# The causal mask of a head pair in quarters of the array

## The reference

```python
q = jnp.einsum('bsd,hde->bhse', x, Wq)
k = jnp.einsum('bsd,hde->bhse', x, Wk)
v = jnp.einsum('bsd,hde->bhse', x, Wv)
scores = jnp.einsum('bhse,bhte->bhst', q, k)
causal = jnp.tril(jnp.ones((S, S), dtype=bool))
scores = jnp.where(causal, scores / jnp.sqrt(jnp.float32(E)), jnp.float32(-jnp.inf))
attn = jax.nn.softmax(scores, axis=-1)
out = jnp.einsum('bhst,bhte->bhse', attn, v)
heads = out.transpose(0, 2, 1, 3).reshape(B, S, H * E)
y = x + heads @ Wo
```

## Time and profile before

| | us |
|---|---|
| median of 3 runs | 875.02 |
| lowest, highest | 874.08, 876.87 |
| the profiled execution | 875.58 |
| its span in the trace | 873.7 |
| TensorE busy in it | 739.8 |
| VectorE busy | 615.9 |
| ScalarE busy | 569.6 |
| GpSimd busy | 510.6 |

### The profile page before, as it was taken

The page is one execution under the profiler, slowest core; times in us unless marked ns, Lnnn a source line. Parts: engine busy times, 40 slices in busy tenths (PEclk is TensorE's granted clock), DMA queues, the critical chain, the costliest instruction groups (busy, mean ns, idle before and its releaser), DMA issues. The chain is left out here.

```text
span 873.7 us, 20974 instructions
## 1 busy us (share of the span) xinstructions
PE 739.8 (85%) x7592; PEld 530.6 (61%) x7592; DVE 615.9 (70%) x1275; ACT 569.6 (65%) x1567; POOL 510.6 (58%) x496
## 2 busy tenths in 40 slices
PE   4881777742799999999999999999999999999842
PEld 3661556632566767667667767766766776676631
DVE  1361665653476668758987986897798698779973
ACT  1462666652476777677777777777777777677633
POOL 3552555343065566856675785667568567666831
PEclk9986888866899999999999999999999999999975
DMA  7500000000099998889889998898788878999820
GB/s 187 119 1 0 1 1 2 0 0 1 14 144 150 146 148 145 142 142 141 139 144 137 151 144 142 146 146 147 136 146 140 147 142 148 139 144 154 149 57 23
DMA packets 360614, 94.00 MB, mean 108 GB/s; under 512 B 347584, under 2 KB 360384, under 8 KB 360512
## 3 DMA queue, kind: packets, MB, share of 16 engines
q1 hardware_dynamic: 357248, 90.57, 62.5%
q10 hardware_dynamic: 3264, 2.10, 0.8%
HBM read 6.63 MB, written 2.10 MB: 10 GB/s over the span
## 5 line engine op out<-in xcount | busy, mean ns | idle before, releaser
L1004 POOL TENSOR_TENSOR prob_hl<-prob,prob_hl 128x768 f16<-128x768 f32 (+1 forms) x192 | 347.6, 1810 | 208.0 <-DVE prob_hl L944 207.7
L915 ACT ACTIVATE prob<-wide,neg_max 128x128 f32<-128x128 f32 (+3 forms) x512 | 264.5, 525 | 157.1 <-DVE neg_max L956 157.1
L956 DVE TENSOR_REDUCE neg_max<-wide 128x2 f32<-128x256 f32 (+3 forms) x256 | 204.6, 821 | 116.9 <-PE wide L833 116.3
L828 PE MATMUL wide<-k_sb,q_sb 64*128 64x128 f32 (+3 forms) x1024 | 190.1, 469 | 0.9 <-ACT k_sb L810 0.8
L944 DVE CAST prob_hl<-prob 128x768 f16<-128x768 f32 (+1 forms) x192 | 149.0, 776 | 0.6 <-ACT prob L915 0.5
L853 PE MATMUL bank<-v_hi,prob_t 128*128 128x64 f16 x1280 | 132.6, 193 | 15.2 <-DMA prob_t<-prob_hl 13.0
L855 PE MATMUL bank<-v_hi,prob_t 128*128 128x64 f16 x1280 | 132.6, 193 | 0.0
L854 PE MATMUL bank<-v_lo,prob_t 128*128 128x64 f16 x1280 | 132.6, 193 | 0.0
L853 PEld LDWEIGHTS bank<-v_hi,prob_t 128*128 128x128 f16 x1280 | 115.5, 98 | 21.8 <-issue 14.6
L855 PEld LDWEIGHTS bank<-v_hi,prob_t 128*128 128x128 f16 x1280 | 114.2, 98 | 0.0
L854 PEld LDWEIGHTS bank<-v_lo,prob_t 128*128 128x128 f16 x1280 | 114.0, 98 | 0.0
(11 more groups left out here) (165 smaller groups left out, 1368.7 us busy)
## 6 DMA issues: line engine op xcount, KB each, us to landing
prob_t<-prob_hl SPq DMA_TRANSPOSE x384, 3.2
x_sb<-in_L_attn_a_in_features SPq DMA_DIRECT2D x8, 256.0 KB, 6.8
out_x<-x_done SPq DMA_DIRECT2D x8, 256.0 KB, 2.7
wq_a<-in_L_attn_a_w_q ACTq DMA_DIRECT2D x1, 512.0 KB, 5.5
wk_a<-in_L_attn_a_w_k ACTq DMA_DIRECT2D x1, 512.0 KB, 7.2
wo_a<-in_L_attn_a_w_o ACTq DMA_DIRECT2D x1, 512.0 KB, 8.4
wv_a<-in_L_attn_a_w_v ACTq DMA_DIRECT2D x1, 512.0 KB, 8.2
wq_b<-in_L_attn_b_Wq SPq DMA_DIRECT2D x1, 512.0 KB, 10.0
```

Source lines behind the costliest of these rows:

```text
L828: pe.matmul(dst[:, h, c:c + m], q[e, i * P:(i + 1) * P], k[e, 0:m], start=(i == UNIT_ROWS[u][0]), stop=False)
L915: last = act.activation(prob_2[s][:, at:at + m], score_banks(p, s)[:, h, c:c + m], ACT.Exp, bias=neg_max[p % 2][:, h, i:i + 1], accum_out= ...
L956: last = dve.tensor_reduce(neg_max[p % 2][:, :, i:i + 1], score_banks(p, s)[:, :, c:c + m], AX.X, ALU.max, negate=True)
L1004: pool.tensor_tensor(prob_hl[u][:, w:2 * w], prob_2[u][:, 0:w], prob_hl[u][:, 0:w], ALU.subtract)\
```

## The change

For each diagonal block of a pair the mask enters with four smaller products in place of two whole ones. For the upper 64 query rows of a block, 64 x 64 of the identity times 128 columns of the mask; for the lower 64 rows, 64 x 64 of the identity times 64 columns (the left 64 columns of these rows are never masked). Head 0 uses partitions 0 to 63 of ident_bf and mask_bf, head 1 partitions 64 to 127. So each product uses a quarter of the array: rows by the head, columns by the half of the query rows. mask_bf grows from 128 to 192 columns, since head 1 reads it from column 64 on. The masks of attention a are as before.

```diff
-        mask_bf = sb("mask_bf", [P, P], BF16)
+        mask_bf = sb("mask_bf", [P, P + E], BF16)
...
-                last = pe.matmul(dst[:, c:c + P], ident_bf[:, :], mask_bf[:, :], start=False,
+                last = pe.matmul(dst[:, c:c + P], ident_bf[:, :], mask_bf[:, 0:P], start=False,
                                  stop=(i == UNIT_ROWS[u][-1]))
...
             pool.affine_select(out=mask_bf[:, :], in_=mask_bf[:, :], compare_op=ALU.is_ge, fill=MASKED, base=0,
-                               pattern=[[-1, P]], channel_multiplier=1).then_inc(sem("consts"), 1)
+                               pattern=[[-1, P + E]], channel_multiplier=1).then_inc(sem("consts"), 1)
...
             for i in UNIT_ROWS[u]:
                 c = PAIR_AT[i] + i * P
-                for h in range(2):
-                    last = pe.matmul(dst[:, h, c:c + P], ident_bf[:, :], mask_bf[:, :], start=False,
-                                     stop=(i == UNIT_ROWS[u][-1]))
+                done = i == UNIT_ROWS[u][-1]
+                for rows in range(2):
+                    out = slice(rows * E, (rows + 1) * E)
+                    n = P - rows * E
+                    for h in range(2):
+                        at = slice(h * E, (h + 1) * E)
+                        last = pe.matmul(dst[out, h, c + rows * E:c + P], ident_bf[at, at],
+                                         mask_bf[at, h * E:h * E + n], start=False, stop=done)
             last.then_inc(sem(f"s{u}"), 1)
```

## The result

| | before | after |
|---|---|---|
| median of 20 runs, us | 875.21 | 877.69 |
| lowest, highest, us | 869.74, 877.94 | 876.62, 879.54 |
| profiled execution, us | 875.58 | 877.59 |

The ratio is 1.0026, with a 95% interval from 1.0014 to 1.0037: the change costs 2.3 us (1.2 to 3.2). The direction was forecast, the size was not: 883 was said, and 880 at the least for that case. Quartering the mask is a small loss.

The account below looks back on a forecast made before the run. TensorE was taken to bound the loop: 169 ns a pair, 10.8 us in 64 pairs, times 0.75 for waits gave 8.1 us. Added to the profiled 875.58 that is 883.7, less 0.56 for the median 883.1; range 868 to 899.

Parts of the forecast that it names:

- TensorE bounds the loop: Loop over 64 head pairs: TensorE, idle 12.3 of 564.00 us, sets the pace; added time reaches the end almost whole.
- A switch costs 95 ns: Between products of different array shapes: each change costs 95 ns; quarters add a second one ahead of L853 per unit.
- Rival B: At the masks: going from 64x128 to 64x64 costs nothing, -7.4 us less a quarter for waits, about 870; chance 0.17.
- Quarters run side by side: In each mask block: four quarters take one 128-column product's time, 56 ns, plus 6 ns for further starts.
- Rivals C and E: Mask quarters: C, one head's run in sequence, 890 to 897, chance 0.18; E, all four in sequence, about 930, chance 0.04.
- The load of a quarter: Ahead of a unit's first quarter: 30 ns of load exposed, taken between 10 and 52.
- The sum of a pair: TensorE's mask work over three units: 75 + 75 + 19 = 169 ns more a pair, 10.8 us in 64 pairs.
- A quarter of the added time vanishes in waits: TensorE's waits, mainly at L853: they absorb a quarter of the added time, 10.8 x 0.75 = 8.1 us.
- VectorE at 81% is far from the bound: In the 260 to 824 us window: VectorE, 81% busy, has gaps enough to take its scores later.
- The signal: From masks to VectorE: scores arrive later by the same amount, and VectorE's mask waits grow from 105.5 us.
- Rival D: In the loop: no change that shows, the size near nothing or waits at L853 taking it all; 873 to 878, chance 0.09.
- A: The forecast for the mask products: quarters overlap, one more switch a unit; 883.1 us, own range 880 to 895, chance 0.52.

Follow-up runs that it names:

- the halves: Mask by halves of the array (64 rows, all 128 columns per head, the scores' shape) instead of quarters: 867.18 us against 875.73 before, ratio 0.9907.

## Why the prediction was right and wrong

**TensorE bounds the loop.** Half right. It is the fullest engine, but the step "a nanosecond added reaches the end almost whole" failed. It rested on 551.68 busy us of 564.00. That number hides up to 0.16 us of each wait under the records, and the 20 us of waits lie in a few pairs of each sequence, where the data that the values' products wait for come at VectorE's and the DMAs' pace. The pair of the earlier trace rows, read as 9.15 us of TensorE's row, held 0.22 us of waits: without them it takes 8.93.

**A switch costs 95 ns, and 64x64 is another shape than 64x128.** Right. It stayed ahead of the masks (1.06 us both times), a second one came behind them, and in the halves one of the two went. The rule of the Trainium skill (TensorEngine Tiling (Array Packing), Key Properties), that a change of tiling mode drains TensorE and a change of tile doesn't, agrees: 528 and 525 ns from the last two scores to the mask across a change of shape, 429 without one. Rival B fell.

**Quarters run side by side.** Right: four starts in 10 ns, where I had 6 to 20. Rivals C and E fell.

**The load of a quarter.** 30 ns exposed were forecast. From the first quarter to L858 it is 175 ns in a unit with one block, where 56 + 6 + 95 + 30 gave 187. With 53 ns for the stream of 128 columns and 95 for the switch some 27 are left for the load, which was sized well; the further starts cost nothing. The estimate of 53 ns that was worked out from the Trainium skill (TensorE: Matmul & The Clock Gate, LDWEIGHTS) is not borne out as exposed time. The 10 ns for the first load behind the switch is there, at the first values' product. The sum of a pair was 169 ns and is about 130: some 14 ns a unit less than said, from the starts, the load and a gap ahead of the masks that is 3 ns shorter.

**A quarter of the added time vanishes in waits.** Wrong, and this is the step that made the miss. 8.2 us x 0.75 would have been 6.2 us, still outside what was measured. Between a half and three quarters vanish: a half for whole products that are added, as the runs with one and three of them show (5.1 of 10.8 us, 16.3 of 32.3), and more for the quarters, part of it since their signal comes sooner. I had written that the awaited data come later too, being descended from TensorE's own scores. That was only argued. In pairs 3 to 6 they are made late by VectorE and the DMAs: with both cut, these pairs run at TensorE's 8.93 us.

**VectorE at 81% is far from the bound.** Wrong, and not only by an average. 81% over the window is 0.94 in pair 2 and 0.66 in pair 0, but the share doesn't tell where TensorE waits either (pairs 3 and 6 above); with VectorE's work cut, 10.5 us were freed.

**The signal.** Wrong. The forecast said that the other engines get their scores later by the same amount, and that VectorE's waits for the mask grow. VectorE gets them 22 to 78 ns sooner after the scores, and its waits fell from 105.5 to 101.5 us.

**Rival D** (waits take most of it) was given 0.09 and is the nearest to what happened: 2.3 us, within the 2.6 that I called no change. The measured 877.7 us lies inside the range from 868 to 899, but below the 880 that A began at; the range held it only because it had been stretched down to B, whose mechanism is wrong. That is luck.

What stays open: how the quarters' gap to the half (1.8 us, with an uncertainty of 1 us) is divided between the sooner signal and the waits of pairs 2 and 7 that the added time happened to fill. Pair 2 became 0.03 us shorter though it has 0.13 us more work, which filling alone can't give, so both have a part there.

## What to carry to other kernels

Before a price on the busiest engine is carried to the end, divide the loop into its repeated stages and compare the length of each with the shortest stage that does the same work. What a stage has above it is waiting, and there a price vanishes until the wait is filled. The busy shares of the other engines don't tell it. A cut in one source of waits frees less than it should, because the next takes over. Put small products that accumulate onto a tile in the same array shape as their neighbours; here a shape of its own cost a switch on each side, and which side of the signal it falls on is worth asking, as a switch behind the signal costs TensorE only.

## What the runs showed of the hardware

- Going from one used part of the array to another costs TensorE about 95 ns at the granted clock's upper level between 128x128 and 64x128, either way, and as much between 64x128 and 64x64 and from there back to 128x128. Between scores and masks of the same 64x128 there was none.
- Four 64x64 products start within 10 ns and run side by side, two of them sharing their 64 rows and two their columns. In the second block of unit 0 the two with 64 columns are recorded as starting some 20 ns ahead of the two with 128 columns, though the program has them behind, as if each quarter took its next product when it is free; by these records the strict order of the front part doesn't hold within TensorE. The signal is on one of the 64-column products, and VectorE starts 58 to 59 ns behind the recorded (modelled) end of the 128-column ones in both sorts of unit, but 79 and 103 ns behind that of the product that carries it. So the signal seems to wait for all of them; no run here tests that. From one 128-column quarter to the next in the same place it is 80 ns, where whole products of 128 columns follow each other in 56.
- A transposing DMA on SyncE's queue holds it for 1.24 us (median) for six or eight blocks, with the DMA engines 88% busy, for 1.17 for a single one, with them 45% busy, and for 1.44 for twice the size, with them 81% busy: the issue's time hardly follows the size.
